# The order of work of five engines in a cross-attention loop is written out anew

## What is computed

```python
x = x + xattn(_layernorm(x), ctx, ctx, WQ, WK, WV, WO, mask)
x = x + ffn(_layernorm(x), W1, b1, W2, b2)
# xattn, for each of the 16 heads h:
logits = (Q @ WQ[h]) @ (K @ WK[h]).T / 8 + mask * -1e9
A[h] = softmax(logits) @ (V @ WV[h])          # and then concat(A) @ WO
# ffn: y = quantized linear (W1, b1), exact gelu, quantized linear (W2, b2);
# each linear scales its whole input by one (max - min) / 255
```

## Time and profile before

| | us |
|---|---|
| median of 3 runs | 1081.73 (1081.44 to 1082.54) |
| profiled execution, whole | 1081.73 |
| its span, first to last instruction | 1079.9 |
| TensorE matmul busy | 1019.1 (94%) |
| VectorE busy | 937.4 (87%) |
| ScalarE busy | 862.5 (80%) |
| GpSimd busy | 766.1 (71%) |

### The profile page before, as it was taken

The page is one execution under the profiler, slowest core; times in us unless marked ns, Lnnn a source line. Parts: engine busy times, 40 slices in busy tenths (PEclk is TensorE's granted clock), DMA queues, the critical chain, the costliest instruction groups (busy, mean ns, idle before and its releaser), DMA issues.

```text
span 1079.9 us, 37623 instructions
## 1 busy us (share of the span) xinstructions
PE 1019.1 (94%) x10639; PEld 650.5 (60%) x10639; DVE 937.4 (87%) x2668; ACT 862.5 (80%) x1809; POOL 766.1 (71%) x1106
## 2 busy tenths in 40 slices
PE   3999999999999999999999999999999999997738
PEld 1555566666666666666666666666666666665327
DVE  5776888888898888888888888888888888886997
ACT  3664888888888888888888888888888888886906
POOL 3336778877777887777887778777777777774700
PEclk9999999999999999999999999999999999999969
DMA  8500676666767676666667767666766666673003
GB/s 238 142 1 14 122 141 139 138 138 138 138 138 140 140 140 139 138 138 138 138 139 140 140 136 138 140 138 139 138 138 139 133 137 140 138 144 127 1 0 123
DMA packets 435437, 136.77 MB, mean 127 GB/s; under 512 B 407666, under 2 KB 434390, under 8 KB 435414
## 3 DMA queue, kind: packets, MB, share of 16 engines
q1 hardware_dynamic: 435414, 136.47, 61.1%
HBM read 28.60 MB, written 6.55 MB: 33 GB/s over the span
## 4 chain that ended last, share of the span: by engine, by line
PE 88%; DVE 7%; ACT 2%; issue 1%; DMA 1%; POOL 0%; ACTq 0%; DVEq 0%; SPq 0%; POOLq 0%
PE front L368 21%; PE front L369 19%; PE front L370 19%; PE back L1309 13%; PE front L1287 7%; PE tp L1287 5%; DVE hrange L1138 3%; DVE hrange L1139 3%; DMA xs<-x 1%; PE front L1424 1%; ACT xn L691 1%; PE tp L1424 1%; PE back L1424 0%; PE front L1192 0%; PE front L1213 0%
## 5 line engine op out<-in xcount | busy, mean ns | idle before, releaser
L616 POOL TENSOR_TENSOR hl<-prob,hl 100x361 f16<-100x361 f32 x511 | 428.6, 853 | 74.6 <-ACT hl L748 73.8
L742 ACT ACTIVATE prob<-prob,nmax 100x361 f32<-100x361 f32 x512 | 295.4, 589 | 5.0 <-DVE nmax L985 3.7
L1309 PEld LDWEIGHTS back<-v,pT 128*128 128x128 f16 (+1 forms) x4608 | 167.8, 98 | 32.3 <-issue 9.6
L748 ACT ACTIVATE hl<-prob 100x361 f16<-100x361 f32 x352 | 175.2, 498 | 3.4
L1309 PE MATMUL back<-v,pT 128*128 128x65 f16 (+1 forms) x4608 | 176.9, 193 | 0.8 <-DMA pT<-hl 0.8
L752 ACT ACTIVATE k_h<-front 128x362 f16<-128x362 f32 x256 | 120.5, 471 | 61.8 <-PE front L370 54.2
L368 PE MATMUL front<-ctx_h,wk_h 128*128 128x362 f16 x512 | 164.0, 320 | 2.4 <-DVE v L1045 1.0
L370 PE MATMUL front<-ctx_h,wk_l 128*128 128x362 f16 x512 | 161.7, 316 | 0.0
L369 PE MATMUL front<-ctx_l,wk_h 128*128 128x362 f16 x512 | 161.4, 315 | 0.0
L1045 DVE SCALAR_TENSOR_TENSOR v<-front,v 128x512 f16<-128x512 f32 (+1 forms) x192 | 132.6, 691 | 30.6 <-ACT v L756 29.9
L756 ACT ACTIVATE v<-front 128x512 f16<-128x512 f32 (+1 forms) x192 | 114.4, 596 | 55.4 <-PE front L370 49.8
(11 more groups left out here) (206 smaller groups left out, 2047.4 us busy)
## 6 DMA issues: line engine op xcount, KB each, us to landing
ctx_raw<-ctxT SPq DMA_DIRECT2D x33, 361.0 KB, 3.2
pT<-hl SPq DMA_TRANSPOSE x253, 3.6
xs<-x SPq DMA_DIRECT2D x8, 400.0 KB
q_all<-x SPq DMA_DIRECT2D x32, 100.0 KB
out<-q_all SPq DMA_DIRECT2D x32, 100.0 KB
xb<-out SPq DMA_DIRECT2D x5, 640.0 KB, 8.2
out<-xb SPq DMA_DIRECT2D x25, 128.0 KB, 1.8
q_all<-wq SPq DMA_DIRECT2D x1, 1024.0 KB, 6.8
```

The source lines that it names most:

```text
L616: pool.tensor_tensor(hl[0:T, n % RT, 1, 0:S], prob[0:T, n % RP, 0:S], hl[0:T, n % RT, 0, 0:S], ALU.subtract).then_inc(s_lo, 1)
L742: act.activation(prob[0:T, n % RP, 0:S], prob[0:T, n % RP, 0:S], ACT.Exp, bias=nmax[0:T, n:n + 1], scale=-1.0).then_inc(s_exp, 1)
L748: act.activation(hl[0:T, h % RT, 0, 0:S], prob[0:T, h % RP, 0:S], ACT.Copy).then_inc(s_ha, 1)
L1309: ins = pe.matmul(obank[j % 2][:, n % GH * DV:(n % GH + 1) * DV], pT[0:r, n % RT, part_ * ST + st, :], v2[half][0:r, st, v, n % HT, :], st ...
```

## The change

New due times in all five tables, and with them new orders. The steps themselves, their sizes and their waits are the same. On TensorE, V3 moves from behind K5 to behind K7, WO0 and WO1 come together behind PV0, CT moves behind PV11, V2 ahead of QP2, and PV3 ahead of QP6. On VectorE, NORM1 moves from the end of the turn to behind K1 of the next, MAX0 goes ahead of K3, HV3 ahead of K0. On ScalarE, EXP11 moves from ahead of V5 to behind C1 and Q1 from behind HA10 to behind Q0; on SyncE, OUT0 goes behind DT4; on GpSimd, Q0 ahead of LO11, M0 behind AL0, and LO0 behind Q1. The two hand-written lists of the last turn take over EXP11 and NORM1.

```diff
 PE_STEPS = at(
-    K=(-4.984, -4.872, -3.617, -3.61, 0.002, 1.727, 3.279, 6.846),
-    V=(-2.536, -1.496, -0.268, 2.931, 7.382, 7.641),
-    QP=(-3.414, -3.413, -1.007, -1.006, 3.022, 3.023, 8.317, 8.318),
...
+    K=(-4.725, -4.364, -3.903, -3.739, 0.06, 1.806, 1.865, 2.958),
+    V=(-3.617, -2.623, 0.055, 3.077, 6.811, 6.836),
+    QP=(-3.698, -3.697, 0.056, 0.057, 2.49, 2.491, 9.371, 9.372),
...
 DVE_STEPS = at(
-    K=(-5.893, -5.648, -4.835, -3.797, -0.261, 0.688, 2.418, 4.814),
+    K=(-5.394, -5.248, -2.513, -2.155, 0.519, 1.348, 1.925, 3.674),
...
-    MAX=(-3.586, -3.558, -3.405, -3.008, -1.096, -0.776, 0.566, 0.613, 2.019, 3.178, 4.599, 6.349, 7.567, 8.998,
-        10.111, 10.476),
+    MAX=(-2.253, -1.786, -0.98, -0.598, 0.248, 0.373, 0.602, 1.062, 3.199, 3.682, 5.123, 7.009, 7.8, 8.323,
+        10.619, 12.252),
...
-    NORM=(7.591, 9.855, 13.495, 16.606),
+    NORM=(8.207, 10.759, 15.577, 16.593),
...
 LAST_ACT = [
-    ("HA", 7), ("EXP", 12), ("AH", 0), ("EXP", 13), ("HA", 8), ("EXP", 14), ("HA", 9), ("EXP", 15),
+    ("HA", 7), ("EXP", 11), ("EXP", 12), ("AH", 0), ("EXP", 13), ("HA", 8), ("EXP", 14), ("HA", 9), ("EXP", 15),
...
 LAST_DVE = [
-    ("MAX", 14), ("MAX", 15), ("HV", 4), ("PC", 10), ("DL", 14), ("PC", 12), ("PC", 14), ("PC", 15),
+    ("MAX", 14), ("NORM", 1), ("MAX", 15), ("HV", 4), ("PC", 10), ("DL", 14), ("PC", 12), ("PC", 14), ("PC", 15),
```

More of the change, by code:

```diff
@@ L87 @@
 PE_STEPS = at(
-    K=(-4.984, -4.872, -3.617, -3.61, 0.002, 1.727, 3.279, 6.846),
-    V=(-2.536, -1.496, -0.268, 2.931, 7.382, 7.641),
-    QP=(-3.414, -3.413, -1.007, -1.006, 3.022, 3.023, 8.317, 8.318),
[L91 to L94, removed]
-ACT_STEPS = at(
[L96 to L105, removed]
@@ L106 @@
-DVE_STEPS = at(
-    K=(-5.893, -5.648, -4.835, -3.797, -0.261, 0.688, 2.418, 4.814),
-    V=(-2.725, -2.274, -0.679, 1.492, 6.435, 6.987),
-    WO=(19.53, 20.987),
-    MAX=(-3.586, -3.558, -3.405, -3.008, -1.096, -0.776, 0.566, 0.613, 2.019, 3.178, 4.599, 6.349, 7.567, 8.998,
-        10.111, 10.476),
-    HV=(-1.157, 1.45, 4.284, 7.744, 10.491),
-    NORM=(7.591, 9.855, 13.495, 16.606),
[L114 to L117, removed]
@@ L118 @@
-SP_STEPS = at(
[L119 to L123, removed]
-POOL_STEPS = at(
[L125 to L132, removed]
+    K=(-4.725, -4.364, -3.903, -3.739, 0.06, 1.806, 1.865, 2.958),
@@ new lines @@
+    V=(-3.617, -2.623, 0.055, 3.077, 6.811, 6.836),
+    QP=(-3.698, -3.697, 0.056, 0.057, 2.49, 2.491, 9.371, 9.372),
+    PV=(3.217, 7.941, 7.994, 9.148, 9.495, 9.838, 10.463, 10.741, 11.681, 11.956, 14.378, 15.369, 16.162,
+        16.594, 16.928, 17.45),
+    WO=(19.367, 19.873),
+    CT=(-15.946,))
+ACT_STEPS = at(
+    K=(-4.298, -3.445, -2.165, -1.475, 5.497, 6.791, 6.907, 8.205),
+    V=(0.456, 1.557, 4.357, 8.456, 9.602, 9.621),
+    EXP=(0.217, 2.363, 3.015, 4.057, 5.558, 7.053, 7.261, 7.75, 8.307, 8.569, 9.197, 10.52, 11.587, 12.483,
+        13.111, 14.388),
+    HA=(1.524, 3.362, 4.512, 6.426, 7.465, 8.502, 8.741, 10.435, 12.941, 13.159, 14.858),
+    AH=(11.677, 16.637, 22.615, 22.624),
+    YN=(25.799,),
+    MG=(-1.628,),
+    C=(-5.95, -5.518),
+    Q=(-5.453, -4.903))
@@ new lines @@
+DVE_STEPS = at(
+    K=(-5.394, -5.248, -2.513, -2.155, 0.519, 1.348, 1.925, 3.674),
+    V=(-0.924, -0.497, 0.265, 3.837, 7.054, 7.273),
+    WO=(21.097, 21.273),
+    MAX=(-2.253, -1.786, -0.98, -0.598, 0.248, 0.373, 0.602, 1.062, 3.199, 3.682, 5.123, 7.009, 7.8, 8.323,
+        10.619, 12.252),
+    HV=(0.09, 2.298, 5.028, 8.693, 12.549),
+    NORM=(8.207, 10.759, 15.577, 16.593),
+    CMAX=(-18.443,),
+    CRED=(-15.753,),
+    SCALE=(-12.759,),
+    LN=(21.545, 22.167, 23.79, 24.463))
+SP_STEPS = at(
+    DT=(4.509, 7.284, 7.843, 8.378, 9.429, 16.363, 18.154, 19.549),
+    AD=(23.151, 23.283),
+    CTX=(-20.277,),
+    OUT=(25.575,),
+    X=(16.32,))
@@ L133 @@
+POOL_STEPS = at(
+    LO=(3.007, 3.539, 4.938, 5.403, 6.776, 7.072, 7.078, 7.676, 8.113, 8.972, 12.241, 12.875, 15.043, 15.508,
+        17.07, 17.124),
+    AL=(17.247, 19.713, 21.698, 22.363),
+    C=(-4.967, -3.871),
+    Q=(-3.27, 2.986),
+    RSTD=(25.802,),
+    CS=(-8.407,),
+    M=(18.185,))
 JOBS = {step: t for step, t in PE_STEPS.items() if step[0] in ("K", "V", "WO")}
```

## The result

The changed kernel takes 1098.97 us (median of 4 runs, 1097.84 to 1099.54), the kernel before took 1081.63 in the same session (4 runs, 1081.44 to 1082.54): a ratio of 1.0155 with an interval of 1.0140 to 1.0172, 17.3 us slower. The forecast was 1091.0, within 1081 to 1099: the sign is right and the size about half of what came.

What follows compares the result with a forecast made beforehand. TensorE was taken to set the pace of the loop's 31 turns of 27.30 us. Per turn +0.48 (V1) - 0.18 (V4) = +0.30, times 31 = +9.3 us: 1081.73 + 9.3 = 1091.0, range 1081 to 1099.

Steps and rivals of the forecast that it cites:

- V1's wait: TensorE's V1 waits for VectorE's read of K3, delayed by NORM1 and MAX0 beyond 0.71 slack: +0.48 us per turn.
- V4's gain: On TensorE between WO1 and V4, the wait for VectorE's read of K7 goes: -0.18 us per turn.
- The wait for ctx_l: TensorE's idle of 0.32 in the middle of K0, waiting for GpSimd's ctx_l; left at its size.
- the 0 for WO0: WO0 on TensorE, now behind K7 and V3, got no wait in the sum; 0.1 or less in hand.
- The rival with more waits: Further waits of 0.2 each at WO0, WO1 and V0: +0.90 us per turn, 1109.6 us; chance 0.05.
- the forecast's own test: Prediction is wrong if, among other signs, waits at WO0, WO1 or V0 are larger than V1's.
- QP's regrouping: V2 and PV3 moved around TensorE's QP steps; pairs stay whole, four entries a turn either way: 0.
- The ends: Hand-written last turn takes over EXP11 and NORM1: 0, give or take 0.3 us once; feed-forward part untouched.
- the upper bound of 1099.1: YN0 0.16 late behind GpSimd's row step, V1 at +0.64, 0.1 at WO1: turn +0.56 us.
- The faster one: Rival: no K3 wait at V1, only the 0.18 ahead of V4 saved per turn: 1076.1 us; chance 0.13.
- the cancelling one: Rival: K0 at its lower bound, V1's 0.28 against 0.18: within 2.2 us of no change; chance 0.12.
- TensorE's clock: Expected unchanged at 1.00; the rival has it fall in the loop, giving 1122 us; chance 0.02.

Runs made afterwards that it cites:

- a2: Changed kernel with NORM1 back ahead of LN3 on VectorE and out of the last turn's list: 1085.06 us.
- a1: Changed kernel with MAX0 back behind K3 on VectorE: 1099.08 us.
- b6: Kernel before with NORM1 behind K1 on VectorE and HA4 ahead of K6 on ScalarE: 1076.85 us, ratio 0.9955 to the kernel before.
- a4: Changed kernel with K7 ahead of EXP7 on ScalarE: 1100.84 us.
- b1: Kernel before with K7's read moved ahead of MAX10 on VectorE: 1100.71 us.
- a6: Changed kernel with MAX0 behind K3 and MAX3 ahead of V0's read on VectorE, and V2 behind QP3 on TensorE; NORM1 stays behind K1: 1086.82 us.
- a3: Changed kernel with EXP11 back ahead of V5 on ScalarE and out of the last turn's list: 1099.05 us.
- a5: Changed kernel with MAX0 behind K3 on VectorE and V2 behind QP3 on TensorE: 1096.94 us.
- b5: Kernel before with only NORM1 moved behind K1 on VectorE and into the last turn's list: 1076.69 us, ratio 0.9958 to the kernel before.

## Why the prediction was right, and where it was wrong

**Right: V1's wait, but its size partly by luck.** The forecast was that NORM1 and MAX0 ahead of K3 overdraw its slack and that nothing is gained ahead of K0. The trace shows that: 0.65 for NORM1, 0.51 for MAX0, VectorE idle 0.76 ahead of K0 (forecast 0.5 to 0.8). a2 shows that NORM1 is needed for the wait. The size needs care. The forecast's 0.48 is how much later V1 starts, counted from V5, with K0's own wait unchanged. By that count it is 0.64: VectorE takes K0 0.17 later (5.06 to 5.23 behind V5's end, medians; forecast 0.04), and from there K3's read ends 1.18 later (forecast 1.15), against 0.71 of slack. K0's longer wait takes 0.19 of the 0.64, so 0.463 is left at V1. That it looks like 0.48 comes from one omission, the late ctx_l and C0, which entered twice with opposite signs. a1 shows what I had not seen: undoing MAX0 would not have helped, as V2 had lost its cover as well.

**Right in itself, wrong in the sum: V4's gain.** WO1 to V4 is 0.180 shorter, as forecast. The step that failed is the sentence "The wait for ctx_l follows from V5, YN0, C0, C1, a chain that keeps its order, so I leave it at its size." On ScalarE it does not quite keep its order, since HA7 now stands between C0 and C1, but GpSimd's two steps of ctx_l run back to back in both kernels (1.66 for the two), so that costs nothing there. What changes is the head of the chain. Before, YN0 followed V5 back to back and the row step had 0.05 in hand (531.01, a hop of 0.17, YN0 at 531.23). With V4 0.18 nearer to WO1 the row step came last: YN0 0.14 later against V5, C0 0.18, ctx_l 0.18, and K0's wait +0.193. I had worked this out (0.16 at YN0) and put it among the bounds, at "all hops at one extreme". It needed no extreme: with 0.05 in hand and 0.18 taken, it was the likely case. b6 shows the trade with almost nothing else changed.

**Wrong: the 0 for WO0.** The sum priced WO1, which needs V3 read, and not WO0, which needs K7 read and now has only V3 and PV0 between. The rival with more waits named it, and I gave that rival a chance of 0.05 because the stretch lies 11 us from V1's. It is +0.168, from K7's reader; a4 shows that the wait goes on to WO0 and WO1 when K7 is read sooner, so it is not K7's place alone. QP4 and QP5's +0.045 wait for K5's reader and had no term. The waits at WO0 are smaller than V1's, so by the forecast's own test the main cause stands.

**The zeros that held.** SyncE's and GpSimd's moved steps cost TensorE next to nothing (the weight loads of the PV steps wait 1.9 us in the whole run for DMAs, 1.0 before); QP's regrouping is -0.04 (V2 and PV11 together). The ends gave -0.7 behind the loop and -0.9 ahead of it, where I had 0, give or take 0.3.

**The sum again.** 0.463 + 0.193 + 0.168 + 0.045 - 0.180 - 0.044 = 0.645. Against my 0.30, K0 makes 0.19 of the difference, WO0 0.17. The time, 1098.97, is at the upper bound of 1099.1, and its main terms are those of that bound: V1 in all 0.64 later behind V5, as in that bound, with WO0's 0.168 in place of 0.1 for WO1. I had called that bound every hop at one extreme; it was nearly the case itself, and the time stays within the range's 1099 by 0.03 us, which is luck.

**The other rivals.** The faster one needed K3 in time, the cancelling one K0 at its lower bound; neither was so. TensorE's clock did not fall: 1.00 over the 863.90 us. In b1, where TensorE is busy for only 817.44 of 840 us, the granted clock of that stretch is 1.00 as well. The Trainium skill, "TensorE: Matmul & The Clock Gate", section "A second HAM failure mode: psum-queue depth-cycling", would have micro-idles between groups of matmuls, with PSUM banks cycled, make it swing between its two levels; the traces here do not agree, at waits of 0.46 us a turn in the changed kernel and 0.73 us in b1.

**Open.** Which earlier step makes K7's and V3's readers late at WO0 was not traced further than a4 goes; and no run put back the whole early part of the changed VectorE list, so the 0.24 per turn that a6 keeps over the kernel before is accounted for by steps (QP4, K0, less WO1) and not tested. The times without an interval are single ones, and the changed kernel's own runs spread over 1.7 us, so differences of 2 us among them (a1, a3, a4, a5) rest on the turns and not on the times.

## What to carry to other kernels

When engines run their lists in order, a step moved later is free only up to the slack of the next reader behind it: add up what now stands ahead of each read that frees a bank, from the last idle time of that engine on, and look at the step after it too, since an unpaid wait goes to the next one. A wait that ends on the way of a long chain may be where that chain's slack shows; before counting its removal as a gain, follow the chain to its end and ask what arrives second. Move one step at a time: here one of the changed places alone, NORM1's, made the kernel 0.4% faster (b5), and the whole set made it 1.55% slower.

## What the runs showed of the hardware

A swap of two neighbouring steps of 0.5 us on one engine cost 0.64 us per turn (b1), more than either of them lasts, because four engines' lists passed it on. Going over to the QP steps, whose weights use 64 rows, cost TensorE 0.08 to 0.10 us: PV11 takes 0.367 ahead of QP2 and 0.273 ahead of another step, V3 1.390 ahead of QP4 and 1.294 ahead of PV0, K6 1.017 ahead of QP4 and 0.933 ahead of PV0. Leaving them cost 0.09: the second QP of a pair takes 0.558, the first 0.470. That the 64 rows are the reason was not tested. And waits of up to 0.73 us in each turn of 28 us left the granted clock at 1.00.
